# A graph layer with a routed FFN on one core: two of GpSimd's waits for PE are left out

## What is computed

```python
xn = layernorm(x)
xp = (xn @ W).reshape(n, 4, 64)
a_src, a_dst = einsum(xp, att_src), einsum(xp, att_dst)       # per node and head
alpha = leaky_relu(a_src[src] + a_dst[dst], 0.2)              # edges and self loops
ex = exp(alpha - amax[dst]); w = ex / segment_sum(ex, dst)[dst]
x = x + elu(segment_sum(xp[src] * w[..., None], dst).reshape(n, 256) + bias)
z = layernorm(x)
weights = z @ wr + br;  sel = top_k(weights, n // 2)[:-1]
y = (gelu(z @ w1 + b1) @ w2 + b2) * weights                   # 256 -> 1024 -> 256
x = x + z;  x[sel] += y[sel]
```

## Time and profile before

| | us |
|---|---|
| runs, median of 3 (lowest to highest) | 2601.36 (2600.11 to 2602.53) |
| the profiled execution | 2596.49 |
| its span, first to last instruction | 2594.7 |
| POOL busy | 1555.7 (60%) |
| of it the 1566 gathers | 1514.7 |
| PE busy | 1966.2 (76%) |
| DVE busy | 1586.9 (61%) |
| ACT busy | 736.6 (28%) |

### The profile page before, as it was taken

The page is one execution under the profiler, slowest core; times in us unless marked ns, Lnnn a source line. Parts: engine busy times, 40 slices in busy tenths (PEclk is TensorE's granted clock), DMA queues, the critical chain, the costliest instruction groups (busy, mean ns, idle before and its releaser), DMA issues.

```text
span 2594.7 us, 33117 instructions
## 1 busy us (share of the span) xinstructions
PE 1966.2 (76%) x9575; PEld 1652.3 (64%) x9576; DVE 1586.9 (61%) x3512; ACT 736.6 (28%) x1506; POOL 1555.7 (60%) x1628
## 2 busy tenths in 40 slices
PE   8934777877777867878777776877777777887787
PEld 6723666756666756756666665666666666666665
DVE  4555665655655665666566565666565565666576
ACT  5600232222232232233232222233222232223233
POOL 2366666666666666666666666666666666666630
PEclk9967888888888888878888888888888888888988
DMA  7754444444444444444444444444444444444447
GB/s 240 222 143 123 131 135 120 136 135 119 133 137 118 131 138 121 133 135 131 123 133 132 119 135 126 126 135 133 117 138 130 124 133 128 126 135 132 116 164 303
DMA packets 155424, 362.45 MB, mean 140 GB/s; under 512 B 46501, under 2 KB 73793, under 8 KB 154114
## 3 DMA queue, kind: packets, MB, share of 16 engines
q0 software_dynamic: 75232, 208.59, 29.4%
q1 hardware_dynamic: 72978, 140.11, 16.4%
q10 hardware_dynamic: 7184, 13.41, 1.4%
HBM read 323.09 MB, written 38.89 MB: 140 GB/s over the span
## 4 chain that ended last, share of the span: by engine, by line
POOL 35%; issue 26%; PE 19%; another core or an unknown queue 8%; DVE 6%; DMA 3%; POOLq 2%; ACT 1%; DVEq 0%; SPq 0%; ACTq 0%
POOL rows L674 35%; PE ag_ps L1009 11%; PE ag_ps L897 3%; DMA rows<-node_rows,ends 3%; PE y_ps L995 2%; DVE rows L1347 2%; DVE base L1546 1%; POOLq L393 1%; PE h_ps L977 1%; PE tr_ps L923 0%; PE xl_ps L923 0%; DMA base<-in_x 0%; DVE oh L1307 0%; DVE zl L1328 0%
## 5 line engine op out<-in xcount | busy, mean ns | idle before, releaser
L674 POOL DMA_INDIRECT rows<-node_rows,ends x1566 | 1514.7, 967 | 864.2 <-issue 617.5
L1009 PE MATMUL ag_ps<-rows,oh 128*128 128x260 f32 x3518 | 1005.7, 456 | 516.6 <-DVE rows L1347 401.5
L1009 PEld LDWEIGHTS ag_ps<-rows,oh 128*128 128x128 f32 x3518 | 809.1, 233 | 682.9 <-issue 366.0
L1347 DVE TENSOR_TENSOR rows<-rows,xl_ps 128x512 f32<-128x512 f32 (+3 forms) x392 | 503.2, 1346 | 29.4 <-issue 18.3
L1326 DVE TENSOR_TENSOR zz<-rows,edge_dm 128x72 f32<-128x72 f32 x98 | 22.9, 233 | 805.0 <-DMA rows<-node_rows,ends 797.9
L802 ACT COPY rows<-rows 128x780 f32<-128x780 f32 x97 | 81.7, 842 | 1109.6 <-DMA rows<-node_rows,ends 1109.6
L977 PE MATMUL h_ps<-xnT,w1s 128*128 128x256 f32 x1568 | 365.7, 385 | 14.0 <-issue 13.8
L995 PE MATMUL y_ps<-w2s,hT 128*128 128x256 f32 x1568 | 357.8, 380 | 3.8 <-issue 1.9
L977 PEld LDWEIGHTS h_ps<-xnT,w1s 128*128 128x128 f32 x1568 | 300.9, 193 | 60.3 <-issue 19.2
L995 PEld LDWEIGHTS y_ps<-w2s,hT 128*128 128x128 f32 x1568 | 298.5, 191 | 50.6 <-issue 3.5
L1307 DVE TENSOR_TENSOR oh<-xl_ps,dloc 128x2304 f32<-128x2304 f32 x98 | 250.0, 2551 | 0.2
(11 more groups left out here) (236 smaller groups left out, 1393.2 us busy)
## 6 DMA issues: line engine op xcount, KB each, us to landing
dbc<-dst SPq DMA_DIRECT2D x97, 576.0 KB
rows<-node_rows,ends POOLq DMA_INDIRECT x1566
selfr<-node_rows SPq DMA_DIRECT2D x98, 130.0 KB
base<-in_x SPq DMA_DIRECT2D x14, 896.0 KB, 4.8
base<-in_x SPq DMA_DIRECT2D x49, 256.0 KB
ffn_rows<-yb ACTq DMA_DIRECT2D x48, 256.0 KB
node_rows<-base SPq DMA_DIRECT2D x13, 910.0 KB, 4.9
out<-base SPq DMA_DIRECT2D x3, 1024.0 KB, 12.8
```

The source lines that it names most:

```text
L674: pool.indirect_dma_start(out=rows[:, b, t, :], out_offset=None, in_=table, in_offset=bass.IndirectOffsetOnAxis(ap=ends[:, b, t, 0:1], axi ...
L1009: product = nc.tensor.matmul(ag_ps[b][:, 0:ROW], oh[:, b, t, :], rows[:, b, t, :], start=(t == 0), stop=False)
L1347: nc.vector.tensor_tensor(v, v, e, ALU.mult).then_inc(scaled[k], 1)
```

## The change

`follow` loses its first and its last wait, and the call that was made for the last one alone goes too. The waits for the three sums, the carry and the loads stay.

```diff
     FREED = 6
-    LOOKED_UP, SUMMED, SECOND_LAYER = 4, (8, 11, 13), TILES - 2
+    SUMMED = 8, 11, 13
     COLS = 8
...
             def follow(w, started):
 
-                if started == LOOKED_UP:
-                    wait_apart(pool, (lk_ok, w + 1))
                 for k in range(GROUPS):
                     if started == SUMMED[k]:
                         wait_apart(pool, (freed[k], w))
-                if started == SECOND_LAYER and known(w, 5) and not (isinstance(w, int) and w == NW - 1):
-                    wait_apart(pool, (y_ok, w - 4))
...
                     wait_apart(pool, (carry_ok, w))
-                    follow(w, TILES - 2)
```

## The result

The change makes the kernel slower: 2991.75 us in the median of 5 runs (2983.68 to 2996.17), where the kernel before took 2600.11 (2595.76 to 2602.53, 5 runs). The ratio is 1.1502, 95% interval 1.1489 to 1.1515: 391.6 us more. The forecast was 2529 us in a range up to 2660, so both its sign and its range were wrong.

What follows compares the result with a forecast made beforehand. POOL's gathers, with stops at waits, were taken as the bound. The profiled 2596.5 us less 72 us gives 2524.5; with the runs' median 4.9 us above the profiled one, 2529 us, range 2495 to 2660.

Steps and rivals of the forecast that it cites:

- What is late next: the wait for the first sum: Before a block's 9th gather: the first sum comes 18.5 us after POOL's restart, its queue runs dry at 19.8 us.
- the middle that I took: Gain per block between two estimates, 1.02 us and 0.59 us; over 90 blocks 92 and 53 us, taken as 72 us.
- PE and DVE have the same busy time.: Sign of being right: in the same part of the loop, busy time of PE and DVE stays unchanged.
- Why, no row tells: Remark that stops come mostly nine gathers or more after the last stop, for a reason no profile row gives.
- the stop: At a short wait, POOL can idle until its gather queue runs dry and a landing more; about 3 us idle.
- The two waits that the change removes hold 75 of 129.: Of 129 POOL idle times over 1.2 us in blocks 6 to 96, 39 stand at lookups, 36 at the second layer.
- One stop a block: Main case: after the change POOL stops once a block, at the first sum; 2495 to 2580 us, chance 0.50.
- ACT's carry waits less: Sign of being right: ACT's carry, which waited 1016.0 us in all for a block's gathers, waits less.
- DVE's collisions, up to 31 us: Gathers meeting DVE's bf16 comparison last longer; at most 31 us given back, kept inside the range only.
- Two stops a block: Rival: POOL waits at the first sum and stops at the second; +57 us, 2658 us, slower; chance 0.30.
- Stops by count: Rival: POOL stops every 11 or so gathers whatever it waits for; no change, 2601 us; chance 0.12.
- No stops at all: Rival: sums ready in time, PE's own work bounds; about 20.5 us a block, 337 us less, 2265 us; chance 0.08.

Runs made afterwards that it cites:

- both_left_out_2: The change itself, both waits left out, with masked loads, against the kernel before on kind B: 2217.20 against 2234.70 us, ratio 0.9922.
- own_landing_3: The change, plus POOL waiting before a block's 5th gather for its own first four to land, against the kernel before, kind B: 2656.8 us, ratio 1.1882.
- lk_only_3: Kernel before with only the second-layer wait left out, masked loads, kind A: 2575.49 against 2577.05 us, ratio 0.9994.
- y_only_4: Kernel before with only the lookup wait left out, masked loads, kind A: 2626.11 against 2598.85 us, ratio 1.0115.
- control: Kernel before with a mask over three loaded counts, against the kernel before on kind B: 2238.35 against 2235.67 us, ratio 1.0011.
- own_landing_4: The change, plus POOL waiting before a block's 5th gather for its own first four to land, against the kernel before, kind A: 2599.96 against 2577.05 us, ratio 1.0089.

## Why the prediction was wrong

- **"What is late next: the wait for the first sum", due 18.5 us after the restart.** This step failed. It took PE's chain as given, with the same second layer, hidden layer and lookups between the sums as before. In its place the first sum came about 29 us after the restart (the gathers at 1204.75 and 1233.93, each released by it, are 29.18 us apart), because PE was held for 10 us in the lookups. The other half of the step was right: POOL's queue ran dry 19.7 us after the restart, and 19.8 was worked out. I had priced POOL's idle time there at 2.88 us in place of 3.90 a block (3.10 by the middle that I took); it is 8.6 in the mean, less the ordinary 0.3 that is 4.4 us above 3.90, and in 90 blocks the 396 us of the profile after. That single term turns -72 us into the loss.
- **"PE and DVE have the same busy time."** True for DVE (1588.7, 1586.9 before). PE is at 2015.0 after 1966.2 with the granted clock at 0.80 after 0.86 in the 90 blocks. I take the clock for an effect of PE's idling: on one chip of kind B, rests of POOL alone took it from 0.913 to 0.844 (both_left_out_2, own_landing_3). As a cause it is too small, 48.8 us more of PE's busy time against 391.6. But busy time was the wrong thing to watch: it was PE's idle time that grew.
- **"Why, no row tells" of the stop.** I had seen the hold-up and taken it for POOL's own. In the earlier trace rows PE's last 14 lookups, ACT's carry and POOL's sequencer all go on within 0.3 us of 351.2; I read only POOL's part and made it a price for each wait. In that kernel the lookups take over 1.2 us in 28 of 91 blocks, and in these they end 2.0 to 2.6 us after the last gather of the row, as after the change. That on kind B the same waits make 11 rests in place of 130 shows that the stop belongs to the kind of chip and not to the wait; that it is the same thing as PE's hold-up is argued from these numbers, not tested by itself.
- **"The two waits that the change removes hold 75 of 129."** The count was right within one (38 and 36 of 130, behind 290 us), the use of it wrong. With one of the waits left out, 125 rests remain of 130, at other waits (lk_only_3: 370 us, y_only_4: 408 us, 391 before). "One stop a block" did come true in the change, 92 of them, all at the first sum, as foretold; each takes 8.6 us and not 3.2. Of the signs of being right one more came true, and it means little: ACT's carry waits less, 903.9 us after 1109.6.
- **DVE's collisions, up to 31 us.** Nothing: a gather takes 962 ns, 967 before. The collisions were there already: behind 290 us, 89 of DVE's 91 bf16 comparisons met a gather before the change, and all 91 after it. The gathers beside them took 1.13 us in the mean before and 1.11 after. The rule that the prediction took from the Trainium skill's page "SBUF — State Buffer", section "SBUF: two separate sides", changes nothing in the time here. I called one lengthened gather agreement with it, and that was too much: it had begun before DVE's operation, and of the 104 gathers that met one, 50 took no longer than 1.1 us.
- **The rivals.** Two stops a block (2658 us) had the sign but not the mechanism: behind 290 us there is not one rest at a second sum. Stops by count (2601 us) was closest to the truth for each wait alone: 0.9994 and 1.0115 on kind A. No stops at all (2265 us, 20.5 us a block) is what happens on kind B, where the change takes 2217 us at 20.24 us a block and the kernel before (control) 20.52: without a hold-up the waits for the sums are met in time, as that rival worked out. I had no case in which an engine other than POOL is held.

The cause is settled in part. Shown: the loss appears on kind A alone; it needs both waits gone; a rest of POOL unrelated to PE takes it back to 1.009; it does not hang on the lookups, nor on the bytes, nor on the loading of code. Open: whether instructions or descriptors in a row count, whether the pause helps or the landing of the gathers, where in the row the hold-up begins for each engine, what holds the engines, and why chips differ.

## What to carry to other kernels

A wait between a stream of gathers and its consumer can be worth more than its idle time: before leaving one out, look at what the other engines do while POOL runs on, and above all for idle time put down to "issue" that ends when the gathers land. On the chips of kind A here, rows of more than about 9 gathers held PE and ACT up, in one kernel DVE too and earlier, and one of two short waits was enough to keep the time. Leave them out one at a time: the second-layer wait alone gave 1.0% on kind B and cost nothing on kind A, the only version here that was at least as fast as the kernel before on both; both together gave 0.8% or lost 15%, by the chip.

## What the runs showed of the hardware

- Two kinds of chip, three met of each in the experiments: the same kernel takes 2235 to 2236 us or 2577 to 2599 us, steadily within 0.3% on one chip but for the one execution named above. One chip of kind B was met twice, 53 minutes apart, and was of its kind both times.
- On kind A, 10 or more gathers without a rest can bring the steps of PE's queue to 1.4 to 2.8 us each (four of five of 413 steps over 1 us between lookups of the changed kernel) until 2.3 to 3.5 us after the last gather of the row has ended; on kind B more than a thousand gathers in a row do nothing of the kind (both_left_out_2).
- The gather's price on POOL is 0.95 us and 0.30 us to the next whatever it moves: 969 ns in the mean for 128 bytes a row, 961 and 962 for 1040 bytes (the change on either kind), 930 for half the rows.
- A rest until a block's first four gathers have landed takes 4.8 us on kind B (437 us in 91), and 2.8 us on kind A (258 us in the 91 at the same place of own_landing_4).
